# Projections spread over all eight steps of batch 0, routing moved beside batch 1, and zero rows written to the free slots alone

## The chip, the core and the metric

The kernel runs on one core of a Trainium2 chip. Its engines are TensorE (PE), VectorE (DVE), ScalarE (ACT), GpSimd (POOL) and SyncE (SP), which issues most DMAs. Each engine works off its own instructions in the order in which they are written and waits on semaphores; nothing reorders them. The metric is device time of one execution in microseconds.

## What is computed

Input x has 4 batches of 512 tokens with 256 features. The block computes `x + s * silu(f)`:

```python
xn = _layernorm(x, axis=-1)
s = _L0_attn_ref(xn, ...)
g = _silu(_L0_ffn_ref(xn, ...))
x = x + s * g
```

`s` is a gated recurrence: after an RMS norm, projections give q and k (128 wide), a decay a (16 heads of 8), v and g (256 wide). The state follows

```python
S = S * jnp.exp(gt)[..., None] + kt[..., None] * vt[..., None, :]
ot = jnp.einsum('bhk,bhkd->bhd', qt, S)
```

over the 512 tokens. Its output is normalised per head, gated by silu(g), multiplied by Wo and added; a gated MLP (704 wide) follows. `f` is a mixture of 16 experts (224 wide) of which a softmax router picks 4 for each token.

## The kernel before

**Attention.** Tokens run along the free dimension, 512 of a batch at once. A batch p needs eight projection outputs, numbered in the order Z (decay), K, V0, V1, LG (router logits), Q, G0, G1. Each is one PSUM bank of a rotation of three (`bank_of`), written by six f16 matmuls, high and low parts being kept apart (`triple`, L315). ScalarE takes out Z, K, Q, G0 and G1, VectorE V0, V1 and LG. V goes to `v_scratch` in DRAM and comes back copied over partitions as `vrep`. One recurrence step (a, u) of the eight of a batch a treats two value columns: VectorE multiplies `kv` (L951) and runs two scans `st` (L959), GpSimd multiplies by q (`product`, L529), TensorE sums over k (`read_out`, L1247). Step u's scans wait for product u-2, so the four engines form a ring. Before a batch is projected its rows are normalised by GpSimd (`normed_rows`, L510), turned by TensorE (`turn_rows`, L1215) and split into `anT` by ScalarE and VectorE (`high_rows`, `low_rows`). The decay also needs a sum by GpSimd (`decay_sum`), behind four passes of ScalarE.

**Order.** It is written out by hand. A prologue loads and splits the weights and projects batch 0. Then batch 0's steps run with the projections of batches 1 to 3 spread over them by one table: after step u come the outputs up to `STEP_ENDS[u]`.

```python
STEP_ENDS = [7, 11, 14, 17, 20, 24, 24, 24]
```

After `FIRST = 6` steps VectorE begins routing: some 35 small operations in a chain, between which `recurrences_beside_routing` puts one piece of a recurrence each (batch 0's steps 6 and 7, batch 1's 0 and 1). At the end `route_ready` says in which slot of `rows_scratch` each token's row goes for each of its four experts, and `name_tiles` says which expert owns each of 80 tiles of 128 slots. Then `turns` runs a pipeline: in iteration `it` batch it does its recurrence (a), batch it-1 its heads, Wo and second norm (b), batch it-2 its MLP (c). GpSimd scatters two of 64 groups of 128 rows in each turn that has a b, from b = 0 on. Slots that no token fills have to be zero: ScalarE issues 16 DMAs (`zero`, L636) that clear all 10240 slots during batch 0's steps, and scatters wait for them.

**Experts.** SP loads the gate and up weights, then waits for the last turn of `an2` (`tpn_ready`) and for all scatters, loads the first 16 tiles' rows (`load_rows`, L452), and then the down weights `wd` in two DMAs (`load_down`, L448). TensorE turns the first two tiles' rows before the last batch's W2 products, does the first tile's gate and up products, waits for both `wd` loads, and goes through the 80 tiles:

```python
gate_up(0, 0, e_first)
pe.wait_ge(s["wd_in"], 32)
tiles(0, True, False)
```

GpSimd adds each tile's output to `y_scratch` by an indirect DMA (L586), and a short tail combines both branches.

## Time and profile before

| what | us |
|---|---|
| median of 3 runs (lowest, highest) | 575.49 (574.5, 575.81) |
| profiled execution, its own time | 574.92 |
| its span, first to last instruction | 572.9 |
| busy: TensorE, VectorE, GpSimd, ScalarE | 429.3, 345.0, 304.7, 230.9 |
| one kv (L951), one scan (L959) on VectorE | 1.212, 1.210 |
| one v copy (L927) on VectorE | 0.688 |
| one product (L529), one decay sum (L515) on GpSimd | 2.352, 1.272 |
| 24 router matmuls (L315, 128x16), 8 turns (L1215) on TensorE | 0.75, 1.09 |
| granted TensorE clock, mean | 0.897 of full speed |

Busy time is the time in which an engine executes; where TensorE's clock is granted at half speed (1.2 instead of 2.4 GHz) the same matmuls are longer. "Idle before" in a row is the time in which the engine did nothing ahead of that instruction, with the one that ended it. DMAs have rows of their own queue (SPq, ACTq), which show the issue, not the transfer.

### The profile page before, as it was taken

What the parts mean: (1) busy time and instruction counts of PE and PEld (TensorE: products, weight loads), DVE (VectorE), ACT (ScalarE), POOL (GpSimd) and SP (SyncE); (2) the same over time, 40 slices, a digit from 0 to 9 for tenths busy, and PEclk for the clock granted to TensorE, in tenths of its full rate; (3) what the DMA queues carried; (4) which work ended last, traced back from release to release, by engine and by line L of the source; (5) the groups of instructions that cost most, each with busy time, mean ns of one, the idle gap of its engine ahead of it and who ended that gap; (6) DMA issues with size and microseconds to landing.
All of it is one profiled execution on the core that took longest, in us unless ns stands there. A gap on an engine that the chain in (4) does not pass through costs nothing.

```text
span 572.9 us, 8861 instructions
## 1 busy us (share of the span) xinstructions
PE 429.3 (75%) x2170; PEld 254.9 (44%) x2171; DVE 345.0 (60%) x613; ACT 230.9 (40%) x521; POOL 304.7 (53%) x230
## 2 busy tenths in 40 slices
PE   2479970313568798699889989999999999999400
PEld 1134320101223354255465557767767767677200
DVE  4665867999989979985755633333333333333065
ACT  0526642300133132122554525556655656566221
POOL 4052695146768468576720006656566656666535
PEclk9989996655759899899999999999999999999855
DMA  8334998745535234232988845666666666664493
GB/s 265 110 111 160 304 330 279 270 150 171 186 123 185 89 126 151 106 114 65 357 288 238 176 149 85 112 101 114 103 112 112 112 102 110 111 85 57 55 318 121
DMA packets 78616, 90.42 MB, mean 158 GB/s; under 512 B 7704, under 2 KB 66808, under 8 KB 78584
## 3 DMA queue, kind: packets, MB, share of 16 engines
q1 hardware_dynamic: 47584, 54.82, 31.6%
q0 software_dynamic: 14592, 19.47, 20.0%
q10 hardware_dynamic: 16408, 15.73, 8.5%
q8 instruction: 16, 0.26, 0.2%
q14 instruction: 16, 0.13, 0.1%
HBM read 50.66 MB, written 39.34 MB: 157 GB/s over the span
## 4 chain that ended last, share of the span: by engine, by line
PE 54%; DVE 19%; issue 9%; DMA 8%; POOL 4%; ACT 2%; ACTq 2%; SPq 0%; POOLq 0%; DVEq 0%
PE mm_ps L315 33%; PE sum_ps L315 12%; DVE st L959 4%; PE turn_ps L1276 3%; DVE kv L951 3%; PE mm_ps L1374 3%; POOL qs L529 2%; DMA rows_scratch<-zrow 2%; DMA eb<-n_L_ffn_expert_bias_dram 2%; PE sum_ps L1247 2%; DVE w_gu L1181 2%; DMA vrep<-v_scratch 1%; DMA y_scratch<-y,X 1%; ACTq L636 1%; DVE ghead L1111 1%
## 5 line engine op out<-in xcount | busy, mean ns | idle before, releaser
L586 POOL DMA_INDIRECT y_scratch<-y,X x80 | 124.3, 1554 | 126.7 <-ACT y L815 96.6
L315 PE MATMUL mm_ps<-w_gu,xT 128*128 x480 | 103.9, 352 | 1.6 <-DVEq L1159 1.5
L529 POOL TENSOR_TENSOR qs<-st,q_sb 128x1024 f32<-128x1024 f32 x32 | 75.4, 2356 | 49.0 <-DVE st L959 24.3
L1071 DVE TENSOR_TENSOR xT<-turn_ps,xT 128x256 f16<-128x256 f32 x80 | 33.9, 425 | 88.0 <-ACT xT L726 88.0
L315 PE MATMUL sum_ps<-wd,hT 112*128 x320 | 82.4, 380 | 0.0
L558 POOL DMA_INDIRECT rows_scratch<-rows,slot_u x64 | 64.0, 1001 | 27.2 <-issue 15.1
L959 DVE TENSOR_TENSOR_SCAN st<-sum_ps,kv 128x512 f32<-128x512 f32 x64 | 75.1, 1210 | 1.0
L315 PE MATMUL mm_ps<-an2T,w 128*128 128x512 f16 x264 | 65.1, 403 | 13.6 <-DVE h_mlp L1080 11.1
L1247 PE MATMUL sum_ps<-qs,sumk 128*32 128x512 f32 x128 | 38.2, 710 | 38.5 <-POOL qs L529 37.2
L315 PEld LDWEIGHTS mm_ps<-w_gu,xT 128*128 128x128 f16 x480 | 46.6, 97 | 33.0 <-issue 2.7
L1164 DVE SCALAR_TENSOR_TENSOR h<-mm_ps,X,sl 128x224 f32<-128x224 f32 x80 | 36.1, 451 | 40.9 <-ACT sl L799 40.9
L315 PEld LDWEIGHTS sum_ps<-wd,hT 112*128 112x128 f32 x320 | 54.3, 190 | 4.7 <-issue 0.2
L815 ACT ACTIVATE y<-sum_ps,X 128x256 f32<-128x256 f32 x80 | 38.0, 474 | 44.3 <-PE sum_ps L315 44.3
L799 ACT ACTIVATE sl<-mm_ps,X 128x224 f32<-128x224 f32 x80 | 35.8, 447 | 43.4 <-PE mm_ps L315 43.4
L315 PE MATMUL mm_ps<-anT,w_a 128*128 128x512 f16 x168 | 43.0, 414 | 11.2 <-DVE anT L912 9.2
L315 PEld LDWEIGHTS mm_ps<-an2T,w 128*128 128x128 f16 x264 | 26.3, 103 | 54.1 <-issue 16.6
L315 PE MATMUL mm_ps<-w,h_mlp 128*128 128x256 f32 x192 | 47.8, 394 | 1.0 <-DVE h_mlp L1080 1.0
L951 DVE TENSOR_TENSOR kv<-vrep,mm_ps 128x1024 f32<-128x1024 f32 x32 | 38.8, 1212 | 5.6 <-ACT mm_ps L677 4.1
L315 PEld LDWEIGHTS mm_ps<-w,h_mlp 128*128 128x128 f32 x192 | 33.9, 189 | 14.5 <-issue 10.0
L732 ACT ACTIVATE sg<-mm_ps 128x512 f32<-128x512 f32 (+1 forms) x24 | 14.3, 597 | 46.8 <-PE mm_ps L315 46.8
L1276 PE MATMUL turn_ps<-ident,X 128*128 128x128 f32 x160 | 30.7, 274 | 2.5 <-issue 2.5
L315 PEld LDWEIGHTS mm_ps<-anT,w_a 128*128 128x128 f16 x168 | 16.9, 105 | 34.9 <-issue 17.8
(165 smaller groups left out, 533.4 us busy)
## 6 DMA issues: line engine op xcount, KB each, us to landing
vrep<-v_scratch SPq DMA_DIRECT2D x64, 256.0 KB
rows_scratch<-zrow ACTq DMA_DIRECT2D x16, 685.0 KB, 11.7
X<-rows_scratch SPq DMA_DIRECT2D x80, 137.0 KB, 2.6
w_gu<-y_scratch SPq DMA_DIRECT2D x16, 256.0 KB, 6.1
y_scratch<-zrow ACTq DMA_DIRECT2D x6, 640.0 KB, 5.9
w_gu<-in_L_ffn_gate_proj_dram SPq DMA_DIRECT2D x16, 224.0 KB, 6.8
w_gu<-in_L_ffn_up_proj_dram SPq DMA_DIRECT2D x16, 224.0 KB, 7.1
wd<-in_L_ffn_down_proj_dram SPq DMA_DIRECT2D x1, 3136.0 KB, 17.4
```

Of the source, the lines that this page charges most:

```text
L315: last = nc.tensor.matmul(out_ap, lhsT, rhs, start=(n == 0), stop=(n == len(pairs) - 1))
L529: nc.gpsimd.tensor_tensor(qs[:, u % 2, :, :], st[:, u % 2, :, :], pair_bc(q_sb[:, TOK(a)]), ALU.mult).then_inc(s["qs_ready"], 1)
L558: nc.gpsimd.indirect_dma_start(rows_dram, bass.IndirectOffsetOnAxis(ap=slot_u[:, j, t:t + 1], axis=0), rows[:, t, :], None).then_inc(s["sc ...
L586: nc.gpsimd.indirect_dma_start(y_dram[u % 2], bass.IndirectOffsetOnAxis(ap=X[:, u, TOKEN_C:TOKEN_C + 1].bitcast(U32), axis=0), y[:, u, :], ...
L799: nc.scalar.activation(sl[:, u % 2, :], M[u % 2][:, 0:I], ACT.Silu, scale=X[:, u, SCALE_C:SCALE_C + 1])\
L815: nc.scalar.activation(y[:, u, :], sum_ps[:, u % 2, 0:D], ACT.Copy, scale=X[:, u, bass.ds(e + WEIGHT_C, 1)])\
L951: nc.vector.tensor_tensor(kv[:, r, :, :], vrep[:, r, :, :], pair_bc(K_BANK), ALU.mult).then_inc(s["kv_ready"], 1)
L959: nc.vector.tensor_tensor_scan(st[:, r, j, :], A_BANK, kv[:, r, j, :], 0.0, ALU.mult, ALU.add).then_inc(s["st_ready"], 1)
L1071: nc.vector.tensor_tensor(xT[:, u % 2, 1, :, :].rearrange("p c n -> p (c n)"), PS[u % 2][:, 0:KC * P], xT[:, u % 2, 0, :, :].rearrange("p ...
L1164: nc.vector.scalar_tensor_tensor(out=h[:, u % 2, :], in0=M[u % 2][:, I:2 * I], scalar=X[:, u, SCALE_C:SCALE_C + 1], in1=sl[:, u % 2, :], o ...
L1247: last = nc.tensor.matmul(O0[rows_at:rows_at + QUARTER, :], sumk[:, off:off + QUARTER], qs[:, u % 2, j, :], start=(dd % PER == 0), stop=(d ...
L1276: last = nc.tensor.transpose(PS[u % 2][:, n * P:(n + 1) * P], X[:, u, n * P:(n + 1) * P], ident[:, :])
```

## The change

1. The outputs' order is V0, V1, Z, K, LG, Q, G0, G1, and batch 0's projection waits for each output's own weights (`LOW_PARTS`) instead of all. Loads are split over more semaphores; five small loads move from ScalarE's queue to SP's. VectorE computes only batch 1's scales ahead of the recurrence; batches 2 and 3 follow in its steps 0 and 1, and GpSimd's rows for them after its products 0 and 1. Value loads of a batch's first four steps wait for the first half of v alone.
2. `STEP_ENDS` spreads the 24 outputs over all eight steps. `FIRST` is 8, and beside routing stand batch 1's steps 0 to 3. The counting matmuls move to batch 1's turn 2, ScalarE's exponential behind batch 0's second half.
3. The 16 clearing DMAs are gone. VectorE computes the numbers of the 2048 free slots (`pad_u`, nine small operations), and GpSimd writes `zrow` to them by 16 indirect DMAs. Scatters begin at batch 0's turn 4; batch 3's turns 0 to 3 hold five scatters and four of the new DMAs each.

```diff
@@ -275,31 +280,40 @@
-        Z_OUT, K_OUT, V0_OUT, V1_OUT, LG_OUT, Q_OUT, G0_OUT, G1_OUT = range(8)
...
+        V0_OUT, V1_OUT, Z_OUT, K_OUT, LG_OUT, Q_OUT, G0_OUT, G1_OUT = range(8)
+        LOW_PARTS = {V0_OUT: 2 * KC, V1_OUT: 2 * KC, Z_OUT: 3 * KC, K_OUT: 3 * KC, LG_OUT: 3 * KC + 1, Q_OUT: 4 * KC + 1,
+                     G0_OUT: 5 * KC + 1, G1_OUT: 5 * KC + 1}
...
-        STEP_ENDS = [7, 11, 14, 17, 20, 24, 24, 24]
+        STEP_ENDS = [4, 7, 10, 13, 16, 19, 22, 24]
@@ -318,6 +332,7 @@
+        SCATTER_FROM = 4
@@ -379,12 +394,24 @@
-            for w, col in ((Wv, VC), (Wg, GC)):
-                sp.dma_start(wa_raw[:, :, col:col + D], w.rearrange("(c p) n -> p c n", p=P)).then_inc(s["wa_in"], 16)
+            sp.dma_start(wa_raw[:, :, VC:VC + D], Wv.rearrange("(c p) n -> p c n", p=P)).then_inc(s["wv_in"], 16)
             for w, col in ((Wq, QC), (Wk, KCOL)):
-                sp.dma_start(wa_raw[:, :, col:col + QK], w.rearrange("(c p) n -> p c n", p=P)).then_inc(s["wa_in"], 16)
-            for c in range(1, B):
+                sp.dma_start(wa_raw[:, :, col:col + QK], w.rearrange("(c p) n -> p c n", p=P)).then_inc(s["wqk_in"], 16)
+            sp.dma_start(wa_raw[:, :, GC:GC + D], Wg.rearrange("(c p) n -> p c n", p=P)).then_inc(s["wg_in"], 16)
+            load_x(1)
...
+                sp.dma_start(bz[:, :], strided(bkg2, 0, [[1, KD], [KD, H], [1, 1]])).then_inc(s["bz_in"], 16)
+                for c in range(KC):
+                    sp.dma_start(bgT[:, c:c + 1], strided(bg, c * DH, [[1, DH], [HD, H], [1, 1]])).then_inc(s["bg_in"], 16)
...
+            for c in range(2, B):
                 load_x(c)
+            with nc.allow_non_contiguous_dma(reason="a few hundred numbers"):
+                sp.dma_start(ln2[:, :], ln2_w.rearrange("(c p) -> p c", p=P)).then_inc(s["late_in"], 16)
+                sp.dma_start(eb[:, :], expert_bias.rearrange("(a e) -> a e", a=1).to_broadcast((P, E))).then_inc(s["late_in"], 16)
@@ -409,9 +436,8 @@
-                if u == 0:
-                    for c in range(2):
-                        sp.wait_ge(vt_out[c], 16 * (b + 2))
+                if u % 4 == 0:
+                    sp.wait_ge(vt_out[u // 4], 16 * (b + 2))
@@ -452,7 +477,7 @@
-            sp.wait_ge(s["scatter"], 16 * NT * TOP)
+            sp.wait_ge(s["scatter"], 16 * (NT * TOP + NPAD))
@@ -541,17 +568,23 @@
+                if u == 0:
+                    pool.wait_ge(s["ln_ready"], 3)
+                if u < 2:
+                    for t in range((u + 2) * TPB, (u + 3) * TPB):
+                        normed_rows(t)
+                else:
+                    mlp_weights((u - 2) // 3, (u - 2) % 3)
@@ -559,20 +592,30 @@
+            def scatter_pads(n):
+                for _, i in zip(range(n), pads):
+                    nc.gpsimd.indirect_dma_start(
+                        rows_dram, bass.IndirectOffsetOnAxis(ap=pad_u[:, i:i + 1], axis=0),
+                        zrow[:, :], None).then_inc(s["scatter"], 16)
             def step_fn(a, b, c, u):
                 if a is not None:
                     if u == 0:
                         pool.wait_ge(s["evac_act"], len(ACT_NTH) * a + ACT_NTH[Q_OUT])
                     product(a, u)
-                if b == 0 and u == 0:
+                if b == 0 and u == SCATTER_FROM:
                     pool.wait_ge(s["route_ready"], 1)
-                    pool.wait_ge(s["zero_fill"], 16 * NT)
-                if b is not None:
+                if b == 1 and u == 0:
+                    pool.wait_ge(s["pads_ready"], 1)
+                if b is not None and (b > 0 or u >= SCATTER_FROM):
                     scatter(2)
+                if b == B - 1 and u < U // 2:
+                    scatter(3)
+                    scatter_pads(-(-NPAD // (U // 2)))
@@ -603,33 +646,36 @@
             nc.scalar.preload_act_table_set("natural_log_exp_and_others")
-            act.wait_ge(s["wa_in"], 64)
-            act.wait_ge(s["small_in"], 16 * NSMALL)
-            act.wait_ge(s["wv_ready"], 1)
+            act.wait_ge(s["ln1_in"], 16)
+            act.wait_ge(s["wqk_in"], 32)
             for c in range(KC):
-                for out_ap, in_ap in wparts(c, 0):
-                    nc.scalar.activation(out_ap, in_ap, ACT.Copy, scale=ln1[:, c:c + 1]).then_inc(s["wprep_act"], 1)
...
             act.wait_ge(s["wz_ready"], 1)
...
+            act.wait_ge(s["wv_ready"], 1)
+            for c in range(KC):
+                nc.scalar.activation(dh_view(c, 0, VC), dh_raw(c, VC), ACT.Copy,
+                                     scale=ln1[:, c:c + 1]).then_inc(s["wprep_act"], 1)
@@ -697,14 +746,8 @@
-                    zero(rows_dram[t * (SLOTS // NT):(t + 1) * (SLOTS // NT)], "zero_fill")
                 if u == 4:
                     value_half(0, 0)
-                if u == 5:
-                    act.wait_ge(s["ex_in"], 1)
-                    nc.scalar.activation(ex[:, :, :], prod[:, :, :], ACT.Exp).then_inc(s["exp_ready"], 1)
-                    act.wait_ge(s["exp_ready"], 1)
-                    nc.scalar.preload_act_table(ACT.Silu)
@@ -716,6 +759,10 @@
             value_half(0, 1)
+            act.wait_ge(s["ex_in"], 1)
+            nc.scalar.activation(ex[:, :, :], prod[:, :, :], ACT.Exp).then_inc(s["exp_ready"], 1)
+            act.wait_ge(s["exp_ready"], 1)
+            nc.scalar.preload_act_table(ACT.Silu)
@@ -928,15 +985,24 @@
+            qk_low(1)
+            dh_low(VC, 2 * KC)
             low_rows(0)
+            decay_low()
+            router_low()
+            qk_low(0)
+            dve.wait_ge(s["bz_in"], 16)
+            nc.vector.tensor_scalar(bz_neg[:, :], bz[:, :], -1.0, None, ALU.mult).then_inc(s["bz_neg"], 1)
+            take_out(0, V0_OUT)
+            dh_low(GC, 3 * KC + 1)
+            take_out(0, V1_OUT)
+            row_scales(0, TPB)
+            take_out(0, LG_OUT)
             dve.wait_ge(s["const_pool"], 1)
             step(nc.vector.tensor_scalar(head_m[:, :], head_i[:, :], H - 1, None, ALU.bitwise_and))
             nc.vector.tensor_scalar(sumk[:, P - H:P], head_m[:, :], 0.0, KS, ALU.is_equal, ALU.mult).then_inc(s["const_dve"], 1)
-            for c in range(1, B):
-                statistics(c)
-            for i in range(OUTS):
-                take_out(0, i)
-            scales(TPB, NT, TPB + NT)
+            statistics(1)
+            scales(TPB, 2 * TPB, 3 * TPB)
             low_rows(1)
@@ -962,19 +1028,27 @@
-            FIRST = 6
+            FIRST = U
+            BESIDE = 4
             for u in range(FIRST):
                 for _ in recurrence(0, u):
                     pass
+                if u == 0:
+                    row_scales(TPB, 2 * TPB)
+                    statistics(2)
+                    statistics(3)
+                if u == 1:
+                    scales(2 * TPB, NT, 6 * TPB)
+                    row_scales(2 * TPB, NT)
                 for p, i in outs_at(u):
                     if turned_before(p, i):
                         low_rows(turned_before(p, i))
                     take_out(p, i)
             def recurrences_beside_routing():
-                for a, u in ((0, FIRST), (0, FIRST + 1), (1, 0), (1, 1)):
-                    yield from recurrence(a, u)
+                for u in range(BESIDE):
+                    yield from recurrence(1, u)
@@ -1036,6 +1115,14 @@
+            of_e = lambda ap: ap.rearrange("p (a e) -> p a e", a=1).to_broadcast((P, NPAD, E))
+            step(nc.vector.tensor_tensor(past, of_e(pads_to[:, :]),
+                                         pad_no[:, :].rearrange("p (i a) -> p i a", a=1).to_broadcast((P, NPAD, E)), ALU.is_le))
+            step(nc.vector.tensor_tensor(past, past, of_e(held[:, :]), ALU.mult))
+            step(nc.vector.tensor_reduce(pad_f, past, AX.X, ALU.add))
+            step(nc.vector.tensor_tensor(pad_f, pad_f, pad_no[:, :], ALU.add))
+            nc.vector.tensor_copy(pad_u[:, :], pad_f).then_inc(s["pads_ready"], 1)
@@ -1219,6 +1306,8 @@
+                if p == 0:
+                    pe.wait_ge(s["wprep_dve"], LOW_PARTS[i])
@@ -1259,12 +1347,6 @@
-                if u == U - 1:
-                    pe.wait_ge(s["m16_ready"], 1)
-                    pe.wait_ge(s["evac_act"], len(ACT_NTH) * B)
-                    sel = M16[:, :, :].rearrange("p t e -> p (t e)")
-                    nc.tensor.matmul(M[0][:, 0:NT * E], before16[:, :], sel, start=True, stop=True)
-                    nc.tensor.matmul(M[0][:, NT * E:2 * NT * E], ones16[:, :], sel, start=True, stop=True).then_inc(s["cum_ready"], 1)
@@ -1308,6 +1390,12 @@
+                if a == 1 and u == 2:
+                    pe.wait_ge(s["m16_ready"], 1)
+                    pe.wait_ge(s["evac_act"], len(ACT_NTH) * B)
+                    sel = M16[:, :, :].rearrange("p t e -> p (t e)")
+                    nc.tensor.matmul(M[0][:, 0:NT * E], before16[:, :], sel, start=True, stop=True)
+                    nc.tensor.matmul(M[0][:, NT * E:2 * NT * E], ones16[:, :], sel, start=True, stop=True).then_inc(s["cum_ready"], 1)
```

GpSimd, from batch 2's turn 6 to the first add of an expert tile, before:

```order
L529 TENSOR_TENSOR qs<-st,q_sb 128x1024
L558 DMA rows_scratch<-rows,slot_u 10240x274 x2
L529 TENSOR_TENSOR qs<-st,q_sb 128x1024
L558 DMA rows_scratch<-rows,slot_u 10240x274 x2
L529 TENSOR_TENSOR qs<-st,q_sb 128x1024
L558 DMA rows_scratch<-rows,slot_u 10240x274 x18
L586 DMA y_scratch<-y,X 2176x256 x16
```

and after the change:

```order
L591 DMA rows_scratch<-rows,slot_u 10240x274 x2
L556 TENSOR_TENSOR qs<-st,q_sb 128x1024
L591 DMA rows_scratch<-rows,slot_u 10240x274 x7
L597 DMA rows_scratch<-zrow,pad_u 10240x274 x4
L591 DMA rows_scratch<-rows,slot_u 10240x274 x5
L597 DMA rows_scratch<-zrow,pad_u 10240x274 x4
L591 DMA rows_scratch<-rows,slot_u 10240x274 x5
L597 DMA rows_scratch<-zrow,pad_u 10240x274 x4
L591 DMA rows_scratch<-rows,slot_u 10240x274 x5
L597 DMA rows_scratch<-zrow,pad_u 10240x274 x4
L591 DMA rows_scratch<-rows,slot_u 10240x274 x4
L629 DMA y_scratch<-y,X 2176x256 x16
```

The block between the last product (`qs`) and the first `y_scratch` holds 18 DMAs before and 42 after; 16 of these take `zrow`.

TensorE, from the turn of batch 1's rows on, before:

```order
L1215 MATMUL turn_ps<-ident,rows 128x128 x8
L315 MATMUL mm_ps<-anT,w_a 128x512 x24
L315 MATMUL mm_ps<-rw,anT 128x16 x24
L315 MATMUL mm_ps<-anT,w_a 128x512 x6
L1215 MATMUL turn_ps<-ident,rows 128x128 x8
L315 MATMUL mm_ps<-anT,w_a 128x512 x30
L1247 MATMUL sum_ps<-qs,sumk 32x512 x2
L315 MATMUL mm_ps<-anT,w_a 128x512 x6
L315 MATMUL mm_ps<-rw,anT 128x16 x24
L315 MATMUL mm_ps<-anT,w_a 128x512 x6
L1247 MATMUL sum_ps<-qs,sumk 32x512 x2
```

and after:

```order
L1302 MATMUL turn_ps<-ident,rows 128x128 x8
L329 MATMUL mm_ps<-anT,w_a 128x512 x24
L329 MATMUL mm_ps<-rw,anT 128x16 x24
L329 MATMUL mm_ps<-anT,w_a 128x512 x6
L1302 MATMUL turn_ps<-ident,rows 128x128 x8
L329 MATMUL mm_ps<-anT,w_a 128x512 x6
L1336 MATMUL sum_ps<-qs,sumk 32x512 x2
L329 MATMUL mm_ps<-anT,w_a 128x512 x18
L1336 MATMUL sum_ps<-qs,sumk 32x512 x2
L329 MATMUL mm_ps<-anT,w_a 128x512 x12
L329 MATMUL mm_ps<-rw,anT 128x16 x24
L1336 MATMUL sum_ps<-qs,sumk 32x512 x2
```

The rows with 24 router matmuls mark LG. Batch 1's projection keeps its place behind the turn, but the second turn (batch 2) is now followed by one output instead of five ahead of the first read-out, and three outputs stand between read-outs from there on.

VectorE, from batch 0's step 0 to step 2, before:

```order
L951 TENSOR_TENSOR kv<-vrep,mm_ps 128x1024
L959 SCALAR_TENSOR_TENSOR st<-sum_ps,kv 128x512 x2
L927 COPY vt<-mm_ps 128x512 x2
L921 TENSOR_TENSOR lg<-mm_ps,rows 128x64
L912 TENSOR_TENSOR anT<-turn_ps,anT 128x512 x2
L951 TENSOR_TENSOR kv<-vrep,mm_ps 128x1024
L959 SCALAR_TENSOR_TENSOR st<-sum_ps,kv 128x512 x2
L927 COPY vt<-mm_ps 128x512
```

and after, first up to the aggregates, then (the reciprocal root lies between) from `shift` on:

```order
L1017 TENSOR_TENSOR kv<-vrep,mm_ps 128x1024
L1025 SCALAR_TENSOR_TENSOR st<-sum_ps,kv 128x512 x2
L921 TENSOR_TENSOR ctmp<-rsq 128x4
L922 SCALAR_TENSOR_TENSOR rows<-ctmp,nhalf 128x4
L901 BN_STATS bst<-xn 128x6 x8
L984 COPY vt<-mm_ps 128x512 x2
L1017 TENSOR_TENSOR kv<-vrep,mm_ps 128x1024
L1025 SCALAR_TENSOR_TENSOR st<-sum_ps,kv 128x512 x2
L907 BN_AGGR mv<-bst 128x2 x8
```

```order
L914 SCALAR_TENSOR_TENSOR shift<-rsq,mv 128x2x8
L921 TENSOR_TENSOR ctmp<-rsq 128x8
L922 SCALAR_TENSOR_TENSOR rows<-ctmp,nhalf 128x8
L978 TENSOR_TENSOR lg<-mm_ps,rows 128x64
L969 TENSOR_TENSOR anT<-turn_ps,anT 128x512 x2
L1017 TENSOR_TENSOR kv<-vrep,mm_ps 128x1024
```

Statistics and scales of batches 2 and 3 now stand between the recurrence's pieces, and the second `anT` split behind them.

## Rows read from the trace of the kernel before

**Rows 1.** Windows: stretch, each engine's busy us (instructions), PE clock, DMA share, GB/s.
```profile
53.04:81.55 28.51, 25.68 (x160) 10.70 (x158) 21.87 (x24) 16.11 (x29) 17.84 (x10) 1.00 0.91 312
81.55:121.65 40.10, 7.80 (x30) 2.34 (x30) 35.09 (x68) 12.00 (x18) 14.61 (x7) 0.65 0.82 275
```

**Rows 2.** Chain that ended last, prologue: start us, us, what.
```profile
6.98 9.39 DMA eb<-n_L_ffn_expert_bias_dram
```

**Rows 3.** Timeline, prologue: start us, us, engine line operation, idle before.
```profile
4.52 1.41 DVE L854 BATCH_NORM_STATS2 bst<-xn 128x6 f32<-128x256 f32 x4 [4.52 <-DMA xn<-in_L_attn_x_dram]
16.46 3.50 ACT L626 ACTIVATE w_a<-wa_raw,ln 128x256 f16<-128x256 f32 x4 [6.80 <-DMA eb<-n_L_ffn_expert_bias_dram]
23.25 7.92 PE L315 MATMUL mm_ps<-anT,w_a 128*128 128x512 f16 x24 [7.83 <-DVE anT L912]
36.14 6.48 POOL L510 TENSOR_SCALAR rows<-xn,rsq,shift 128x256 f32<-128x256 f32 x12 [6.13 <-DVEq L870]
40.67 1.21 DVE L951 TENSOR_TENSOR kv<-vrep,mm_ps 128x1024 f32<-128x1024 f32 x1
```

**Rows 4.** Timeline, projections and read-outs beside batch 0's steps.
```profile
40.85 7.66 PE L315 MATMUL mm_ps<-anT,w_a 128*128 128x512 f16 x24 [2.02 <-issue]
57.68 1.05 PE L1247 MATMUL sum_ps<-qs,sumk 128*32 128x512 f32 x4
58.67 1.47 PE L315 MATMUL mm_ps<-anT,w_a 128*128 128x512 f16 x6
81.55 1.33 DVE L985 TENSOR_TENSOR lg<-lg,eb 128x256 f32<-128x256 f32 x1 [2.47 <-PE mm_ps L315]
```

**Rows 5.** Waits of VectorE, 40 to 166 us: in total, times, longest.
```profile
DVE kv L951 <- ACT mm_ps L677: 4.1, 1, 4.1
```

**Rows 6.** Timeline, after routing; the last row is batch 3's.
```profile
125.03 1.86 DVE L1047 TENSOR_SCALAR tile_expert<-own 1x80 uint32<-1x80 f32 x1
135.02 2.79 DVE L1111 TENSOR_SCALAR ghead<-ghead 128x64 f32<-128x64 f32 x1
135.39 2.35 POOL L529 TENSOR_TENSOR qs<-st,q_sb 128x1024 f32<-128x1024 f32 x1
141.84 1.21 DVE L951 TENSOR_TENSOR kv<-vrep,mm_ps 128x1024 f32<-128x1024 f32 x1
277.48 0.20 DVE L1111 TENSOR_SCALAR ghead<-ghead 128x64 f32<-128x64 f32 x1
```

**Rows 7.** Timeline of GpSimd, end of its attention work.
```profile
269.06 0.96 POOL L558 DMA_INDIRECT rows_scratch<-rows,slot_u  x1 [0.30 <-issue]
270.33 0.96 POOL L558 DMA_INDIRECT rows_scratch<-rows,slot_u  x1 [0.31 <-issue]
288.97 1.23 POOL L558 DMA_INDIRECT rows_scratch<-rows,slot_u  x1 [0.30 <-issue]
```

**Rows 8.** Timeline, from the first row loads to the first expert tile.
```profile
300.45 7.46 SPq L452 DMA_DIRECT2D X<-rows_scratch  x16
321.26 0.60 PE L1276 MATMUL turn_ps<-ident,X 128*128 128x128 f32 x4
322.83 12.00 PE L315 MATMUL mm_ps<-w,h_mlp 128*128 128x256 f32 x48 [0.97 <-DVE h_mlp L1080]
337.55 0.41 PE L1276 MATMUL turn_ps<-ident,X 128*128 128x128 f32 x2
```

**Rows 9.** Page, DMA issues: count, KB each, median us to landing.
```profile
X<-rows_scratch SPq DMA_DIRECT2D x80, 137.0 KB, 2.6
wd<-in_L_ffn_down_proj_dram SPq DMA_DIRECT2D x1, 3136.0 KB, 17.4
rows_scratch<-rows,slot_u POOLq DMA_INDIRECT x64, 3.8
```

**Rows 10.** Windows: the row and down-weight loads, and a busier stretch.
```profile
300.45:326.00 25.55, 23.75 (x107) 13.12 (x106) 15.59 (x19) 12.42 (x18) 0.00 (x0) 1.00 0.95 230
277.00:285.00 8.00, 6.44 (x32) 2.84 (x30) 7.55 (x19) 4.00 (x6) 6.17 (x7) 1.00 1.08 383
```

138 lines of the change are left out of this document (80 added, 58 removed).

## Prediction

> **What bounds the kernel now.** I read the windows by stage first, then the chain that ended last, then the timeline of the stages that the change touches. Three stages follow each other. Beside batch 0's first six recurrence steps TensorE is the busy engine: 25.68 of 28.51 us against VectorE's 21.87 [rows 1]. In the routing stretch VectorE works 35.09 of 40.10 us and TensorE 7.80 [rows 1]. From about 300 us on TensorE hardly stops until the tiles end, so whatever delays its first expert tile (337.55 [rows 8]) moves the end by as much. The prologue is a chain of its own: ScalarE's weight copies wait until 16.46 for the last small load, which was issued at 6.98 and took 9.39 us [rows 2, 3].
>
> All sums are made against the profiled run: span 572.9 us, its own time 574.92, so 2.0 us lie around the span; the median of the runs, 575.49, is 0.57 above it.
>
> **Prologue.** ScalarE's queue now carries four loads instead of nine, and the weights of v are prepared first. VectorE ends the first normalisation at 9.2 as before (statistics at 4.52 [rows 3]), copies wk1T and centres Wv until about 11.7. Then come two v copies by ScalarE at 0.88 each (3.50 for four [rows 3]), one more VectorE remainder (0.5) and anT's two halves (1.3 after the first copy): the first projection starts at about 15.0 instead of 23.25. TensorE gives V0, V1, Z, K in 7.92 us [rows 3] and the router's product 0.75 later, at 23.8. VectorE now starts batch 1's statistics there: 0.4 for the head mask, then the same statistics and scales that took 4.52 to 9.20 for batch 0, 4.7 us, so GpSimd gets batch 1's rows at 28.9. From that start to the first kv it is 40.67 - 36.14 = 4.53 us [rows 3]. First kv at 33.4: **7.3 us earlier**. The small loads that moved to SP's queue (bz, two bgT, ln2, eb) stand ahead of W1, W3, wo and w2 and then of v's store; if they land as late as eb did, 9.4 us after issue, they still come by 17, before their first use. The bounds of this term are 4 and 9.
>
> **Batch 0's steps.** These lose ground. Step 0 costs VectorE a recurrence (3.55: kv 1.21 and two scans of 1.17, as in the table), 0.6 of row scales, 2.7 of statistics for batches 2 and 3 and the two v copies: the second kv at 41.9, its scans end at 45.5. Then stand the scales of batches 2 and 3, 3.5 us, on the path of GpSimd's rows 2, of TensorE's turn and of the remainder of anT: 49.0 + 4.5 = 53.5 for the third kv. TensorE idles about 5 us until 49.2 and restarts at G0 of batch 1 at 51.5. What is left for it until the router's last input: 16 outputs at 1.47 [rows 4] = 23.5, two router products 1.5, one turn 1.1 (table), six read-outs at 1.05 [rows 4] = 6.3, so 32.4. I add 1.8 for restarting at the low level of its clock (24 matmuls took 7.66 after a pause where four groups at 1.47 make 5.9 [rows 4]) and 1.6 for read-out 5. That one waits for GpSimd, which has batch 3's decay sum queued before product 5: Z at 77, four ScalarE passes 2.6, sum 1.3, product 2.35, so 83.3 where TensorE is there at 81.7. The bias add that opens routing starts at 51.5 + 35.8 = 87.3 instead of 81.55 [rows 4]: **5.8 later**, though two more recurrences are then done.
>
> **Routing and what follows.** It kept VectorE from 81.55 to 121.65, 40.1 us with four recurrences beside it [rows 1]. The 4.1 us wait for batch 1's K bank [rows 5] was ScalarE held by issuing zero fills; these issues are gone, about 1.1 of the wait stays while the last g is taken out. Four small operations are added (0.9). So 38.0, **2.1 less**. The five operations that find the free slots add 2.1 behind it. Two recurrences (7.0) no longer follow. Two operations were stretched by a GpSimd product: the last of the tile names took 1.86, the head scale 2.79 against 0.20 in batch 3 [rows 6]. GpSimd will have nothing to do there, since product 3 is long done and product 4 needs step 4: I take 0.2 for each, 4.3 less together (bounds 0 and 5). Sum: 7.0 + 4.3 + 2.1 - 2.1 - 5.8 = **5.5 us**: the kv of batch 1's step 4 at 136.3 instead of 141.84 [rows 6]. From there the order is the old one up to batch 3, so this stage hands on 5.5. The 7.3 of the prologue are inside it, not beside it. Bounds 0 and 10.
>
> For these stretched operations the Trainium skill (SBUF — State Buffer, the section on the two separate sides) says that VectorE and GpSimd share a port pair which one instruction holds to its end. The 2.79 beside a product that starts 0.37 us later and ends with it agrees [rows 6]. The same rule speaks against the change: more scatters run beside VectorE's work, and it could hold GpSimd's descriptors up. The old burst's mean spacing already has that in it; by it rather than by the clean spacing the sum below would be 1.4 us more.
>
> **Free-slot rows at the end of attention.** This part costs. Batch 0's first four turns scatter nothing now, so before batch 3's turns 40 scatters are issued instead of 48; 24 are left, and 16 for free slots come on top: 40 in a row where 16 stood. The 16 start at 269.06, 1.27 apart, the last at 288.97 [rows 7]. Twenty-four more at 1.27 are 30.5 us: the last starts at 319.5 and lands 3.8 later [rows 9], at 323.3. All times here are the old ones; the 5.5 are taken off at the end. SP's row loads wait for all of them; they began at 300.45 [rows 8], when another wait (the last turn of an2) ended. So they start **22.9 later**. The two first rows land at 326.4 (0.47 + 2.6 [rows 9]); TensorE turned them at 321.26 and began W2 at 322.83 [rows 8], now at 327.0: 4.2 of delay. It then stands before its wait for the down weights at 341.7. Those are issued behind 16 row loads (7.46 us) and need 17.4 [rows 8, 9]: 323.3 + 24.9 = 348.2. The second part, 0.45 MB, was issued 14 us after the first; now it is right behind it, 1.9 us at 0.24 MB per us: 350.1. The loads ran at 230 GB/s with the DMA busy 0.95 of the time [rows 10], so nothing hides here. The first tile's turn at 337.55 [rows 8] becomes 350.1: **12.5 later**. After 8 us of idleness I take the 1.8 for the low clock once more (0 to 3). Together 14.3, bounds 10 and 18. The zero fills that go (16 of 685 KB) shorten nothing: their place had one wait of ScalarE, counted above.
>
> Sum: 574.92 - 5.5 + 14.3 = 583.7; beside the median of the runs **584.3 us**.
>
> **Rivals.**
> The weights arrive in time (faster). If the 5.9 MB of rows and down weights moved at 383 GB/s, as another stretch shows [rows 10], they would take 15.3 us and be there at 339 to 340, before TensorE asks. Only the 4.2 of the two first rows would remain: 574.92 - 5.5 + 4.2 = 573.6. It decides from landing before 341.7. Against it: that stretch moved other shapes, and these loads filled the DMA at 230. Chance 0.08. The Trainium skill (DMA: Bandwidth & Descriptors, Bandwidth) gives three quarters of the peak for transfers of 1 MiB and more; an estimate by it is about 10 us for the 3.2 MB that took 17.4 here [rows 9], so the trace disagrees.
>
> The front gives more. Without TensorE's and GpSimd's waits routing could start at 83.9 (51.5 + 32.4) and the tail could cost its lower bound: 574.92 - 8.9 + 10 = 576.0. For it: my walk through the steps has many waits of 1 to 2 us. Chance 0.08.
>
> The burst is hidden altogether: row loads at their old place, 574.92 - 5.5 = 569.4. It would need scatters at half of 1.27; all in the trace stand at that or above. Chance 0.04.
>
> The front gives nothing. The stretched operations stay stretched (4.3) and one more decay sum delays a read-out (1.2): 574.92 + 14.3 = 589.2. For it: GpSimd has two decay sums inside products' way. Chance 0.18.
>
> My forecast has 0.62. Within 0.2% (1.2 us, what a measurement of this kernel can tell) of 575.49 lie most of the second rival: same 0.06; faster 0.12; slower 0.82. The range of 8 in 10 is 577 to 590.
>
> **What would show it.** First projection near 15, first kv near 33, bias add of routing near 87, batch 1's kv of step 4 near 136; the head scale 0.2 there. At the end of attention a block of 42 indirect transfers without a product between them, row loads starting more than 20 us after the last turn of an2, and TensorE with a hole of about 8 us just before the first expert tile, ended by the down weights. I am wrong if that hole is absent or under 3 us, or if batch 1's step 4 comes before 131.

## The result and the profile after

| | before | changed |
|---|---|---|
| median of 4 and 4 runs, us | 575.65 | 586.81 (585.19 to 588.25) |
| ratio | | 1.0197, 95% interval 1.0162 to 1.0231 |
| profiled run, its span, us | 574.92, 572.9 | 585.87, 583.8 |
| mean granted clock | 0.897 | 0.877 |

The changed kernel is slower by 1.6 to 2.3%. The prediction was 584.3 (577 to 590), slower, with 0.82 on it. The span grew by 10.9 us.

The front, from VectorE's timeline of the changed kernel (start, length, engine, line, operation, tiles; in brackets the idle time ahead and what ended it):

```profile
33.78 1.21 DVE L1017 TENSOR_TENSOR kv<-vrep,mm_ps 128x1024 f32<-128x1024 f32 x1
...
87.06 0.42 DVE L1059 TENSOR_TENSOR lg<-lg,eb 128x256 f32<-128x256 f32 x1 [3.04 <-PE mm_ps L329]
...
89.34 1.22 DVE L1017 TENSOR_TENSOR kv<-vrep,mm_ps 128x1024 f32<-128x1024 f32 x1 [1.86 <-ACT mm_ps L723]
...
129.24 0.19 DVE L1134 TENSOR_SCALAR tile_expert<-own 1x80 uint32<-1x80 f32 x1
...
130.60 0.20 DVE L1198 TENSOR_SCALAR ghead<-ghead 128x64 f32<-128x64 f32 x1
...
134.83 1.21 DVE L1017 TENSOR_TENSOR kv<-vrep,mm_ps 128x1024 f32<-128x1024 f32 x1
```

The first kv comes 6.9 earlier than in [rows 3], the bias add that opens routing 5.5 later than in [rows 4], the K bank is waited for 1.86 us instead of 4.1 [rows 5], and the two stretched operations of [rows 6] are at 0.2. The kv of batch 1's step 4 stands 7.0 us before its old place.

GpSimd's timeline where attention ends: the last product, the first indirect DMAs behind it, and the last of them.

```profile
259.22 2.35 POOL L556 TENSOR_TENSOR qs<-st,q_sb 128x1024 f32<-128x1024 f32 x1 [3.54 <-DVE st L1025]
261.72 1.01 POOL L591 DMA_INDIRECT rows_scratch<-rows,slot_u  x1 [0.16 <-issue]
...
264.31 0.96 POOL L591 DMA_INDIRECT rows_scratch<-rows,slot_u  x1 [0.31 <-issue]
...
317.41 0.96 POOL L591 DMA_INDIRECT rows_scratch<-rows,slot_u  x1 [0.30 <-issue]
```

There are 42 in a row, 40 of them from 264.31 to 317.41; in [rows 7] the last one starts at 288.97. What waits for them, in the timeline of SyncE's queue and TensorE:

```profile
320.20 7.47 SPq L477 DMA_DIRECT2D X<-rows_scratch  x16
...
322.48 1.17 PE L1358 MATMUL turn_ps<-ident,X 128*128 128x128 f32 x4 [5.74 <-issue]
...
323.43 14.10 PE L329 MATMUL mm_ps<-w,h_mlp 128*128 128x256 f32 x48
...
327.71 8.71 SPq L473 DMA_DIRECT2D wd<-in_L_ffn_down_proj_dram  x2
...
338.28 0.39 SPq L487 DMA_DIRECT2D xback<-in_L_attn_x_dram  x1
...
339.06 1.30 PE L329 MATMUL mm_ps<-w_gu,xT 128*128 x6 [1.53 <-DVEq L1246]
...
347.66 0.66 PE L1358 MATMUL turn_ps<-ident,X 128*128 128x128 f32 x2 [7.29 <-DMA wd<-in_L_ffn_down_proj_dram]
348.11 2.45 PE L329 MATMUL mm_ps<-w_gu,xT 128*128 x6
```

and its DMA issues in that stretch (KB each, us from issue to landing):

```profile
wd<-in_L_ffn_down_proj_dram SPq DMA_DIRECT2D x1, 3136.0 KB, 17.0
X<-rows_scratch SPq DMA_DIRECT2D x16, 137.0 KB, 3.3
xback<-in_L_attn_x_dram SPq DMA_DIRECT2D x1, 2048.0 KB, 14.1
wd<-in_L_ffn_down_proj_dram SPq DMA_DIRECT2D x1, 448.0 KB, 18.7
```

The row loads go out at 320.20 instead of 300.45 [rows 8]. The products of W2 start 0.6 later than before although the front is 4.8 ahead there, and last 14.10 instead of 12.00 because the granted clock is at its lower level after the pause of 5.74 (0.65 of full speed on the mean from 323.4 to 330, 1.00 in the kernel before). Then TensorE stands 7.29 us before the first expert tile and the down weights end the wait. The tile turns at 347.66 instead of 337.55 [rows 8]. The account of the span: -4.8 (front) + 5.4 (rows) + 2.1 (clock in W2) + 7.3 (down weights) gives +10.0 at the tile's turn, measured 10.1. Behind it 0.8 more comes on top: the first tile's six products take 2.45 instead of 1.31 at the low clock, and a pause of 0.74 that the kernel before has there falls away.

Part of the 7.3 may belong to another load. At 338.28, when W2 has ended, SyncE issues the load of x for the tail (`xback`, 2048 KB) while the down weights are still under way, and it takes 14.1 us, where it took 8.4 in the kernel before, in which they had landed. From 320.20 to 347.66 the DMA engines moved 245 GB/s, that is 6.7 MB, of which the row and down-weight loads are 5.9. An estimate from these: up to 0.8 MB of x, 2 to 3 us, went ahead of the last of the weights. No run issues that load later.

Of the 7.0 gained by batch 1's step 4 only 4.8 are left at batch 3's step 7 (kv 255.41 instead of 260.19). Of the 2.2 lost, 1.9 go at two places: 1.1 at batch 2's step 5 and 0.8 at batch 3's step 5. TensorE's timelines show both, of the changed kernel

```profile
182.39 5.30 PE L329 MATMUL mm_ps<-an2T,w 128*128 128x512 f16 x12 [5.25 <-DVE h_mlp L1167]
...
234.11 5.27 PE L329 MATMUL mm_ps<-an2T,w 128*128 128x512 f16 x12 [4.83 <-DVE h_mlp L1167]
```

and of the kernel before

```profile
189.11 4.34 PE L315 MATMUL mm_ps<-an2T,w 128*128 128x512 f16 x12 [4.73 <-DVE h_mlp L1080]
...
239.71 4.45 PE L315 MATMUL mm_ps<-an2T,w 128*128 128x512 f16 x12 [4.83 <-DVE h_mlp L1080]
```

The same twelve products ran at 1.2 GHz to their end, or nearly so, in the one (granted clock 0.50 from 182.39 to 187.60) and rose to 2.4 GHz on the way in the other, the second time after the same idle time of 4.83. No order of instructions changed there.

The first kv itself is uncertain by a microsecond or two. Nine traces have the changed kernel's prologue: the first 24 projection products start between 15.38 and 15.60 in all of them, take 6.68 to 7.95 us, and the first kv follows at 32.26 to 33.78. Five traces have the prologue of the kernel before: products of 6.84 to 7.92 us, first kv at 38.27 to 40.84. The trace above has the longest of the one (7.95) and [rows 3] the longest of the other (7.92), so the 6.9 compare like with like.

### The profile page after: what moved, and what is told of

Its sections match the earlier page's. It is cut to its first block and busy times, and to the rows that moved or that the text cites. A ratio compares the mean times of both kernels' runs of the same rounds, so it can differ in the third digit from the quotient of the medians.

```text
span 583.8 us, 8897 instructions
## 1 busy us (share of the span) xinstructions
PE 440.6 (75%) x2170; PEld 258.5 (44%) x2171; DVE 343.3 (59%) x638; ACT 230.6 (40%) x523; POOL 324.4 (56%) x247
## 5 line engine op out<-in xcount | busy, mean ns | idle before, releaser
L329 PE MATMUL mm_ps<-w_gu,xT 128*128 x480 | 105.3, 356 | 1.6 <-DVEq L1246 1.5
L329 PE MATMUL mm_ps<-an2T,w 128*128 128x512 f16 x264 | 66.4, 409 | 14.2 <-DVE h_mlp L1167 11.7
L591 POOL DMA_INDIRECT rows_scratch<-rows,slot_u x64 | 65.3, 1021 | 16.6 <-issue 15.9
L1336 PE MATMUL sum_ps<-qs,sumk 128*32 128x512 f32 x128 | 39.5, 700 | 23.5 <-POOL qs L556 23.4
L329 PE MATMUL mm_ps<-w,h_mlp 128*128 128x256 f32 x192 | 49.9, 407 | 0.0
L329 PE MATMUL mm_ps<-anT,w_a 128*128 128x512 f16 x168 | 45.9, 430 | 5.0 <-DVE anT L969 1.9
L329 PEld LDWEIGHTS mm_ps<-w,h_mlp 128*128 128x128 f32 x192 | 35.4, 197 | 14.2 <-issue 10.3
L773 ACT ACTIVATE xT<-turn_ps 128x256 f16<-128x256 f32 x80 | 30.2, 377 | 11.6 <-PE turn_ps L1358 11.4
L1358 PEld LDWEIGHTS turn_ps<-ident,X 128*128 128x128 f32 x160 | 22.6, 146 | 24.9 <-issue 17.4
```

The costliest lines, as they stand in the source:

```text
L329: last = nc.tensor.matmul(out_ap, lhsT, rhs, start=(n == 0), stop=(n == len(pairs) - 1))
L591: nc.gpsimd.indirect_dma_start(rows_dram, bass.IndirectOffsetOnAxis(ap=slot_u[:, j, t:t + 1], axis=0), rows[:, t, :], None).then_inc(s["sc ...
L1336: last = nc.tensor.matmul(O0[rows_at:rows_at + QUARTER, :], sumk[:, off:off + QUARTER], qs[:, u % 2, j, :], start=(dd % PER == 0), stop=(d ...
L1358: last = nc.tensor.transpose(PS[u % 2][:, n * P:(n + 1) * P], X[:, u, n * P:(n + 1) * P], ident[:, :])
```

## The experiments

Twelve runs, on four chips, each chip used at one time only: e1 to e4 on chip 2, e5 to e8 on chip 11, e9 to e11 on chip 1, e12 on chip 3. Which chip the first comparison ran on is not on record. One thing differs between them, and the reading of every run hangs on it. In the first comparison and in e9 to e11 batch 3 runs smoothly beside the indirect DMAs. In all the others TensorE, ScalarE and VectorE nearly stop there. I call that the crawl, and speak of chips with and without it; whether it belongs to the chip or to something else that differed at that time, these runs do not separate. It can be read off one distance: from the kv of batch 3's step 7, written kv(3,7), to the first turn of the last an2 on TensorE. This work is the same in every kernel. "Before beside it" is the kernel before measured together with the run.

| run | indirect DMAs in a row | kv(3,7) | an2 turn | distance | median us | before beside it | ratio (95%) |
|---|---|---|---|---|---|---|---|
| before | 18 | 260.19 | 298.78 | 38.6 | 575.65 | | |
| changed | 42 | 255.41 | 294.11 | 38.7 | 586.81 | 575.65 | 1.0197 (1.0162, 1.0231) |
| e9 | 2 | 262.02 | 300.61 | 38.6 | 575.81 | 575.25 | 1.0007 (0.9983, 1.0030) |
| e10 | 26 | 256.97 | 295.64 | 38.7 | 572.03 | 575.25 | 0.9949 (0.9928, 0.9969) |
| e11 | 6 | 260.54 | 299.14 | 38.6 | 574.95 | 575.25 | 0.9991 (0.9966, 1.0017) |
| e5 | 18 | 260.18 | 309.31 | 49.1 | 586.90 | 585.09 | 1.0040 (1.0004, 1.0075) |
| e7 | 18 | 258.42 | 308.66 | 50.2 | 586.04 | 585.09 | 1.0013 (0.9980, 1.0046) |
| e2 | 23 | 255.49 | 311.58 | 56.1 | 589.06 | 584.85 | 1.0064 (1.0037, 1.0092) |
| e1 | 26 | 253.49 | 313.76 | 60.3 | 591.77 | 584.85 | 1.0101 (1.0069, 1.0132) |
| e12 | 26 | 255.22 | 314.18 | 59.0 | 590.55 | 584.70 | 1.0110 (1.0077, 1.0143) |
| e8 | 26 | 253.80 | 312.69 | 58.9 | 590.50 | 585.09 | 1.0083 (1.0051, 1.0114) |
| e3 | 42 | 253.41 | 333.90 | 80.5 | 609.57 | 584.85 | 1.0402 (1.0360, 1.0445) |
| e4 | 42 | 255.86 | 335.41 | 79.6 | 610.37 | 584.85 | 1.0412 (1.0372, 1.0451) |
| e6 | 42 | 254.83 | 334.07 | 79.2 | 609.86 | 585.09 | 1.0402 (1.0375, 1.0430) |

**e1_gaps and e12_gaps_again**, the changed kernel with its indirect DMAs dealt out otherwise:

```
+            PER_TURN = [[0, 0, 0, 0, 2, 2, 4, 2], [2, 2, 2, 6, 3, 2, 4, 2], [2, 2, 2, 6, 3, 2, 4, 2], [3, 3, 3, 3, 3, 3, 3, 3]]
...
-                    scatter(2)
-                if b == B - 1 and u < U // 2:
-                    scatter(3)
-                    scatter_pads(-(-NPAD // (U // 2)))
+                    spread_rows(PER_TURN[b][u])
```

(`spread_rows(n)` issues rows as long as there are some, then zero rows.)

> The changed kernel with its 80 indirect DMAs (64 of rows, then 16 of zero rows) dealt out anew: 2, 2, 4, 2 in the last four turns of batch 0, then 2, 2, 2, 6, 3, 2, 4, 2 in the turns of batch 1 and of batch 2 (the extra ones where GpSimd stood idle 5.8, 1.9 and 3.5 us in the changed kernel's trace), and 3 in each turn of batch 3, which is left 24 instead of 40. Theory 1 (the block delays everything behind it, the front is a gain): the last of them starts near 294 instead of 317.4, the row loads go out near 296 instead of 320.2, no wait of several us for the down weights stands before the first expert tile, which turns near 333; 586.8 - 10.1 - 4.8 gives 571 to 573, some 4 us faster than the kernel before. Theory 2 (the front gains nothing that lasts, what was lost lies in the clock and in TensorE's work): 580 or more, hole or no hole. Theory 3 (GpSimd has no room in batches 1 and 2, products come late): hole gone, product of step 7 of batch 3 at 263 or later instead of 259.2; 575 to 580.

> The changed kernel with its 80 indirect DMAs dealt out as in the first run of this study (2, 2, 4, 2 in batch 0, 2, 2, 2, 6, 3, 2, 4, 2 in batches 1 and 2, 3 a turn in batch 3), once more, since the crawl of the engines beside the row of indirect DMAs, which two of the three chips show, covered what it was to tell. On a chip without the crawl, theory 1 (the long row cost what the front had gained and more): kv of step 7 of batch 3 at 255.4 as in the changed kernel, last of 26 in a row at 296, row loads near 297, first expert tile at 332.8, 4.8 before the kernel before; ratio 0.990 to 0.994 and time 569 to 572. Theory 2 (the zero rows cost time wherever they stand): no better than with the zero fills back, 572 to 574. On a chip with the crawl: ratio 1.007 to 1.013 as the first time.

Both fell on chips with the crawl, which covers the late row loads: the 571 to 573 of theory 1 were missed by 20 us, and the theories are not decided by the time. Two things can still be read. Seven extra indirect DMAs a batch fit into GpSimd's idle time: kv(3,7) is at 253.49 where e3, with the old dealing on the same chip, has 253.41. And 16 fewer in a row are worth 17.8 us on e1's chip (609.57 - 591.77, e3 standing for the changed kernel, which was not run there).

**e2_even**, as e1 with 3 in every turn.

> The changed kernel with three indirect DMAs in every turn from step 4 of batch 0 on (12 in batch 0, 24 each in batches 1 and 2, 20 in batch 3). One turn of GpSimd with a product and two of them took 4.84 us in the changed kernel's trace, with three it takes 6.1. Eight turns then need 49 us, and eight turns of the second batch stood 49.2 us apart (kv of step 4 of batch 1 at 134.8, of batch 2 at 184.0). Theory 1 (room only in the gaps): short turns of 3.5 to 4.8 us are overrun, products are late in five of eight turns and TensorE and VectorE wait for them, 3 to 8 us are lost against the run with the gaps filled; 575 to 580. Theory 2 (GpSimd is far enough ahead): the same time as with the gaps filled, 571 to 573.

GpSimd's timeline in batch 2:

```profile
181.89 2.37 POOL L556 TENSOR_TENSOR qs<-st,q_sb 128x1024 f32<-128x1024 f32 x1
184.43 1.00 POOL L591 DMA_INDIRECT rows_scratch<-rows,slot_u  x1 [0.17 <-issue]
185.74 0.97 POOL L591 DMA_INDIRECT rows_scratch<-rows,slot_u  x1 [0.30 <-issue]
187.01 0.96 POOL L591 DMA_INDIRECT rows_scratch<-rows,slot_u  x1 [0.30 <-issue]
188.00 2.37 POOL L556 TENSOR_TENSOR qs<-st,q_sb 128x1024 f32<-128x1024 f32 x1
```

A turn takes 6.11 us and GpSimd has no idle time left, as theory 1 says, but kv(3,7) is only 2.0 later than in e1, less than the 3 to 8 expected. The time is 2.7 us shorter than e1's (589.06 against 591.77) all the same: the row at the end has 23 instead of 26, and beside the crawl that counts for more (distance 56.1 against 60.3).

**e3_down_first**, the changed kernel with two row loads ahead of the down weights and fourteen behind.

> The changed kernel, its block as it is, but of the 16 row loads only two go out ahead of the big load of the down weights, the other 14 behind it. The down weights are then issued near 321.3 instead of 327.7. Theory 1 (weights are late because they are issued late): they land near 339, the wait of 7.3 us ahead of the first expert tile is 0 to 1.5, the first tile turns near 341 instead of 347.7; 579 to 581. Theory 2 (bandwidth): the loads of the rows and the weights together take the same time in any order, the hole stays above 4 us; 584 to 587.

Not told: with the crawl TensorE reaches the expert tiles so late that no weights are waited for in any order (609.57; the changed kernel 609.86 in e6). That the hole of 7.3 could be closed this way stays open.

**e4_before_late**, the kernel before with 42 of its 64 indirect DMAs in a row at the end:

```
-                if b is not None:
-                    scatter(2)
+                if b == 1:
+                    scatter(1)
+                if b == 2:
+                    scatter(2)
+                if b == B - 1 and u < U // 2:
+                    scatter(10)
```

> The kernel before with nothing changed but where its 64 indirect DMAs stand: none in batch 0, one a turn in batch 1, two in batch 2, ten in each of the first four turns of batch 3, so that 40 stand in a row at the end, as in the changed kernel. Theory 1 (the block alone makes the tail late): the block starts near 266.5 and its last one near 319 to 322, row loads near 323 to 325, a hole of 7 to 8 us before the first expert tile; 575.6 + 10.1 + 4.8 = 590.5, 587 to 592, slower than the changed kernel, whose front is 4.8 earlier. Theory 2 (the tail is late for something else in the change, the zero rows or the DMA traffic of the front): 576 to 582. Beside it: if the stretched operation on head scales at 135.0 (2.79 us) was stretched by GpSimd's indirect DMA issues, it takes 0.2 here, and kv of step 4 of batch 1 comes 2 to 4 us earlier than 141.8.

The ratio 1.0412 equals within the noise the changed kernel's 1.0402 (e6, on another chip with the crawl). Nothing of the change but the length of the row is in this kernel: the length alone makes such a loss there. The sizes expected were wrong, since the crawl sets the tail and not the row loads. The side question has an answer: the head scale took 1.46, not 0.2, with no indirect DMA near, but beside a product, with which it ends:

```profile
132.67 2.35 POOL L529 TENSOR_TENSOR qs<-st,q_sb 128x1024 f32<-128x1024 f32 x1 [1.14 <-DVE st L963]
133.61 1.46 DVE L1115 TENSOR_SCALAR ghead<-ghead 128x64 f32<-128x64 f32 x1
```

It is so everywhere. Between 90 and 262 us the 14 traces have 37 of these small operations (head scales of 128x64, tile names) that take 0.9 to 3.1 us instead of 0.2 to 0.3. Each of them ends 0.05 to 0.10 after a product of GpSimd, there is none without a product, and none that runs beside a product stays short. In 27 of the 37 the small operation even starts 0.3 to 0.7 before the product's recorded start. The kv of batch 1's step 4 is at 139.10, 2.9 before its place in e5 (141.99), but 2.6 of that stood already at the first kv (38.27 against 40.84).

**e5_before_again, e6_after_again**, both kernels unchanged.

> The kernel before, unchanged, profiled on the chip of these runs, since in the first four runs all engines stood still for 8 to 15 us at a time between 270 and 295 with no work ahead of them, while the 32 expert weight loads ran, and the kernel before took 584.9 in the median beside them instead of 575.5. Theory 1 (instruction supply: one engine has to wait for its next instructions behind the burst of loads): the same kind of stall, of 5 to 12 us in all, stands in this trace too between 270 and 300; about 585. Theory 2 (the stall belongs to the edited kernels): no stall, 575.

> The changed kernel, unchanged, on the chip of these runs. Theory 1 (stall beside the burst wherever an engine runs out of instructions in it): a stall of 8 to 25 us between 262 and 300 in its trace, part of it hidden by the late row loads (they go out at 320 anyway); 590 to 600, ratio 1.01 to 1.03. Theory 2: trace as in the first comparison, 586.8 and ratio 1.02.

The crawl is in both, so no edit makes it. (The same kernel against itself gave 1.0040, with 1.0004 to 1.0075 as interval: a ratio that is half a per cent from 1 says little.) ScalarE in e6:

```profile
270.26 0.60 ACT L779 ACTIVATE sg<-mm_ps 128x512 f32<-128x512 f32 x1 [1.13 <-issue]
271.22 0.95 ACT L832 ACTIVATE w_gu<-w_gu 128x896 f16<-128x896 f32 x1 [0.36 <-DMA w_gu<-in_L_ffn_up_proj_dram]
285.76 0.60 ACT L779 ACTIVATE sg<-mm_ps 128x512 f32<-128x512 f32 x1 [13.59 <-issue]
286.25 1.05 ACT L799 ACTIVATE gs<-g_sb 128x1024 f32<-128x1024 f32 x1
287.20 0.94 ACT L832 ACTIVATE w_gu<-w_gu 128x896 f16<-128x896 f32 x1
316.55 0.60 ACT L779 ACTIVATE sg<-mm_ps 128x512 f32<-128x512 f32 x1 [28.41 <-issue]
```

TensorE in e6:

```profile
275.34 1.78 PE L329 MATMUL mm_ps<-an2T,w 128*128 128x512 f16 x6 [2.58 <-issue]
286.41 2.74 PE L329 MATMUL mm_ps<-an2T,w 128*128 128x512 f16 x6 [9.29 <-issue]
301.27 2.74 PE L329 MATMUL mm_ps<-an2T,w 128*128 128x512 f16 x6 [12.11 <-issue]
317.20 2.74 PE L329 MATMUL mm_ps<-an2T,w 128*128 128x512 f16 x6 [13.19 <-issue]
```

TensorE starts 0.65 to 0.75 us after ScalarE's sg (285.76, 316.55) and VectorE's gating (h_mlp, 300.52) start: it is not late itself. Those three are. By the program the first needs a product that ended by 272.8, the second only the sg that ended at 286.4, the third a product that ended at 277.1, and ScalarE was free from 288.1. GpSimd's last indirect DMA starts at 313.42, and from 316.55 on all is smooth again. In the trace of the first comparison the same steps take their normal time beside the same row. The windows of e6 (PE, PEld, DVE, ACT, POOL busy, clock, DMA share, GB/s) show the weight loads end near 295 and the stop go on:

```profile
280.00:290.00 10.00, 2.74 (x6) 0.74 (x6) 0.61 (x1) 2.38 (x3) 7.66 (x8) 0.50 1.08 385
290.00:300.00 10.00, 0.00 (x0) 0.00 (x0) 0.00 (x0) 0.00 (x0) 7.56 (x9) 0.50 0.63 231
300.00:310.00 10.00, 2.74 (x6) 0.74 (x6) 2.88 (x4) 0.00 (x0) 7.56 (x9) 0.50 0.30 110
```

**e7_before_few, e8_gaps_few**, at most 8 of the 32 expert weight loads under way:

```
             for e in range(E):
+                if e >= 4 and e % 2 == 0:
+                    sp.wait_ge(raw_in[e // 2 - 2], 64)
                 load_gate_up(e)
```

> The kernel before, with one thing changed: the queue that issues the 32 expert weight loads of 224 KB waits, before each group of four from the third on, until the group two ahead of it has landed, so that at most 8 are under way instead of all 32. Theory 1 (the instruction supply waits behind the queued loads): no engine stands still for more than 3 us with nothing to wait for; 573 to 577, faster than the kernel before on this chip by 8 to 10. Theory 2 (the stall has nothing to do with the depth of the burst): stalls as before, 585.

> The changed kernel with the indirect DMAs dealt out as in the first run of this study (2, 2, 4, 2 / 2, 2, 2, 6, 3, 2, 4, 2 twice / 3 a turn) and the expert weight loads at most 8 at a time. If both causes are found (theory 1 on the block, and instruction supply behind the burst), nothing late is left and the front's gain stays: row loads near 296, no hole before the first expert tile, 570 to 573, and 4 to 5 us faster than the kernel before with the same throttled loads. If the front's gain is not real: 575 to 578 with both.

No effect: distances of 50.2 (49.1 in e5) and 58.9 (59.0 in e12, 60.3 in e1). Theory 1, that instructions are supplied late because the loads queue so deep, is refuted as far as the depth goes. Nor would it explain e6 after 295. The trace of e6 has two transfers of instructions between 262 and 322, one at about 275 and one between 302 and 303, both just after VectorE has taken up work again (274.60, 300.52), while there are three stops. The Trainium skill (Runtime: NRT & Kernel Launch, Instruction fetch mechanics) says that an engine's instructions are refilled in blocks of 16 KiB by a DMA queue of its own and that crossing such a block is mostly hidden; whether it is here, no run shows.

**e9_before_early**, the kernel before with none of its indirect DMAs in batch 3.

> The kernel before with its 64 indirect DMAs dealt out as 2, 2, 2, 2, 2, 2, 4, 2 in batch 0 and 2, 2, 2, 6, 3, 2, 4, 2 in batches 1 and 2, none in batch 3. In the repeated profile of the kernel before, TensorE, ScalarE and VectorE crawled from 273 to 291 (about 10 us lost) and took up speed again 1.5 us after the last of the 18 indirect DMAs in a row (289.6); in the changed kernel the crawl ended at 317.2, 2.8 us after the last of 42 (314.4). Theory 1 (the crawl hangs on the indirect DMAs in a row beside the weight loads): no wait over 3 us between 262 and 300, row loads near 300, 575 to 577, ratio 0.982 to 0.986. Theory 2 (the burst of weight loads alone makes it): crawl to the end of the loads at 290 as before, 585. Theory 3 (GpSimd has no room in batches 1 and 2): the products come late, 578 to 582.

The chip had no crawl, so theory 1 was not put to the test. On such a chip taking the row away gains nothing: with 2 instead of 18 it takes 575.81, ratio 1.0007. The new dealing loses 1.8 at kv(3,7) (1.1 of it at batch 2's step 5, where TensorE's clock rose late here too), and the profiled span is 1.7 longer; the distance is 38.6 in both.

**e10_fill_back**, the free-slot rows undone: ScalarE's zero fills back, the 16 indirect DMAs of zero rows and their arithmetic out.

> The changed kernel with one of its three parts undone: the zero rows are again written by ScalarE's 16 large zero fills in batch 0, the 16 indirect DMAs of zero rows and the arithmetic for their numbers are out. 26 instead of 42 indirect DMAs stand in a row at the end. Theory 1 (each indirect DMA in the row costs its 1.27 us at the end): 16 x 1.27 = 20 us earlier end of the row, and the part of the crawl that it held: 609.9 - 14 to 20 = 590 to 596. Beside it the arithmetic for the numbers (2.1 us of VectorE at 124) goes, and ScalarE issues 16 fills beside the projections. Rival (the fills, 9 MB, hold up the loads of the values and K bank): 596 to 600.

The chip had no crawl; against the changed kernel's 586.81, measured where before took 575.65, it takes 572.03 where before took 575.25. So this one part costs 14.4 us (586.81 - 572.03 - 0.4 between the two befores), by runs at two times. GpSimd's and TensorE's timelines:

```profile
296.54 0.96 POOL L589 DMA_INDIRECT rows_scratch<-rows,slot_u  x1 [0.30 <-issue]
```

```profile
318.12 0.60 PE L1336 MATMUL turn_ps<-ident,X 128*128 128x128 f32 x4
319.69 12.00 PE L329 MATMUL mm_ps<-w,h_mlp 128*128 128x256 f32 x48 [0.97 <-DVE h_mlp L1145]
333.25 1.31 PE L329 MATMUL mm_ps<-w_gu,xT 128*128 x6 [1.56 <-DVEq L1224]
334.42 0.41 PE L1336 MATMUL turn_ps<-ident,X 128*128 128x128 f32 x2
```

The row starts 1.6 later than the changed kernel's and ends 20.9 earlier, so it is 22.4 shorter, 1.40 for each of the 16. Row loads go out at 299.06, 1.8 after the last turn of an2 has ended: the row still holds them a little, but that is hidden. There is no pause before W2 and no hole before the first tile, which turns 13.2 before the changed kernel's and 3.1 before [rows 8]. These 3.1 are the front's: kv(3,7) is 3.2 before its place in the kernel before, though about 1 of that may be the prologue's clock (24 products in 6.84 here, 7.92 in [rows 3]). The fills cost the front something: VectorE waits for the K bank again,

```profile
94.47 1.22 DVE L1008 TENSOR_TENSOR kv<-vrep,mm_ps 128x1024 f32<-128x1024 f32 x1 [3.91 <-ACT mm_ps L713]
```

and of these 5.1 us (89.34 in the changed kernel) 2.5 are left at batch 1's step 4, since the arithmetic for the free slots is gone too, and 1.6 at kv(3,7), the two groups of twelve products taking 4.94 and 4.45 here instead of 5.30 and 5.27.

**e11_fill_early**, e10 with 6 in a row instead of 26:

> The changed kernel with the zero fills back as in the run before this, and the 64 indirect DMAs dealt out as 2, 2, 4, 2 from step 4 of batch 0, 2, 2, 2, 7, 3, 3, 4, 2 in batches 1 and 2 and 1, 1, 1, 1 in batch 3: the new front without the old tail. Theory 1 (front worth 4.8 to 7 us, row of indirect DMAs the rest): no crawl, row loads near 294 to 296, first expert tile near 331; 569 to 573 and 3 to 7 us faster than the kernel before with none in batch 3. Theory 2 (the front gives nothing): the same time as that kernel. Theory 3 (10 extra indirect DMAs a batch are too many for GpSimd beside the products): 575 to 580.

574.95, ratio 0.9991. By the time alone theory 2 would do as well as theory 3; the trace decides for the third. kv(3,7) is at 260.54, 3.6 later than in e10: nine extra indirect DMAs in each of two batches use up the front's gain, and nothing is won back, since 26 in a row held no engine up.

**The fastest version is e10**, on a chip without the crawl: 0.9949 (0.9928 to 0.9969) of the kernel before. The interval is clear of 1 and the trace shows the gain at the first tile, but it is hardly more than the 0.4% that one kernel differed from itself. It was not run on a chip with the crawl. There its 26 in a row would stand beside e1's, and e1 lost to the kernel before by 1.0%.

## Why the prediction was right

- **Prologue.** 15.0 and 33.4 were forecast for the first projection and the first kv; 15.47 and 33.78 came, 6.9 us earlier instead of 7.3. Second and third kv: 41.9 and 53.5 against 42.07 and 53.76. That the kv agree to 0.4 is in part luck: the sum took 7.92 for the first 24 products, which take 6.68 to 7.95 by where the clock rises. The small loads were no limit, as the sum had it. (The sum's two scans of 1.17, said to be the table's, are 2.34; by the table's 1.210 they are 2.42, which changes nothing.)
- **Bias add** 87.3, measured 87.06, with TensorE as the engine waited for (3.04) and its wait for product 5 (2.50 at 81.63), behind batch 3's decay sum, as forecast.
- **Routing and what follows.** From the bias add to the kv of step 4 I had 49.0 us; it took 47.8. The wait for the K bank was held by the zero fills' issues, as the step said: e10 brings them back and the wait with them (3.91). Tile names and head scale went to 0.2, and the products stretch them, as the step said (37 of 37 cases, under e4).
- **Front handed on unchanged.** Here the step failed. 7.0 was gained at step 4 against 5.5 forecast. The order is the old one from there, but that does not hand the gain on: 2.2 were given back, 1.9 of them at two places where TensorE's clock rose later. 4.8 arrived at the end of attention. The term was right within 0.7 by two errors of opposite sign, which is luck, and the clock is the one to learn from.
- **The row of indirect DMAs.** 42 without a product between them, as forecast; mean spacing of the 40 (317.41 - 264.31) / 39 = 1.36 instead of 1.27, because six of them were stretched to 1.2 to 1.9. The row of the kernel before has such ones too: (288.97 - 269.06) / 15 = 1.33, so "1.27 apart" was its common spacing and not its mean, and the prediction's own 1.4 us for the difference belonged in the sum. The last started 3.4 later than forecast (314.0 with the front taken off): 0.75 because the row began later, 2.7 by the spacing. It landed 2.8 after its start instead of 3.8. Row loads 320.20 against 317.9.
- **Hole before the first tile.** 8.4 forecast, 7.29 measured, ended by the down weights; the smaller second load (448 KB) took 18.7 us and landed last, as reckoned. That the load of x shares the DMA engines with them from 338.28 on was in no term. First tile: 12.5 - 5.5 = 7.0 later forecast, 10.1 measured; the whole: 12.5 + 1.8 - 5.5 = 8.8 forecast, 10.9 measured in the span. The 2.1 too little are 0.7 of front, 1.2 of later first rows (5.4 against 4.2) and 2.1 + 0.8 - 1.8 = 1.1 of clock, less 1.0 of hole.
- **Low clock.** One term of 1.8 was too little and stood at the wrong place: it was put behind the hole, where 0.8 came, and nothing was put on W2, which lost 2.1 after a pause of 5.74 that the sum had reckoned as delay only.
- **Tail in all.** 14.3 forecast; measured 10.9 + 4.8 = 15.7 in the trace, and 14.4 by undoing the part (e10), which also gives the fills back. Both are inside 10 to 18.
- **Rivals.** Weights in time, burst hidden: refuted by the hole and by row loads 19.8 later. Front gives nothing: refuted, 4.8. The front gives more: refuted, since it wanted routing to begin at 83.9 and it began at 87.06; the 7.0 at step 4 came from elsewhere (routing 1.2 shorter than reckoned, bias add 0.24 earlier).
- **Not foreseen.** On three of four chips the kernel before takes 585 us. The changed kernel, run on one of these, takes 610, and the change costs 4.0% instead of 2.0%. There the loss comes with the same row but by another way: the last an2 turn itself is late (334.07), the row loads go out when it has ended (335.74) although the last indirect DMA started at 313.42, and no hole stands before the first tile.

## What to carry to other kernels

Where one engine's DMA issues form a row at the end of a stage, count them and multiply by the spacing in the trace (1.27 to 1.36 us here): 9 MB of zeros less (11.2 filled before, 2.2 written now) cost 16 issues, 22 us of row, and 14.4 us of time. Look at what else waits at that place before shortening it further; on the chip without the crawl 26 in a row cost nothing, 42 did, 6 gained nothing more, while on the others already 18 come with 10 us. Measure a change of this kind on more than one chip, and compare with a run of the kernel before on the same chip.

## What the runs showed of the hardware that was not expected

- **The crawl.** On three of four chips ScalarE and VectorE start late after all that they wait for is there, by 12.3 us in e5 (sg at 290.49, its product done by 276.81 and ScalarE free from 278.18) and by 13.0, 14.2 and 28.4 us in e6, while GpSimd's indirect DMAs stand in a row in batch 3. The distance of the table grows by 10.5 (11.6 in e7), 17.5, 21.7 (20.4, 20.3) and 41.9 (41.0, 40.7) us for 18, 23, 26 and 42 in a row: about 1.27 us, one DMA's spacing, for each beyond the first ten. So it ends with the row, whatever its length. It doesn't hang on the depth of the weight loads (e7, e8), nor on their running at all (e6 after 295). In batches 1 and 2, where products stand between them, two to six do no such harm. What makes the engines slow, and why not on every chip, stays open. So does whether the row makes the crawl or only sets its end: a kernel without a row there was run only on the chip without the crawl.
- **The clock of TensorE** rose in the middle of a group of twelve products in one kernel and at its end or later in the other, the second time after the same idle time of 4.83 us (4.45 against 5.27). In e10 the first of the groups took 4.94 after an idle time of 5.82. So the length of the pause before does not decide it alone. 1.9 us of a gain won upstream were lost by that, with no change of order.
- **A small VectorE operation is held to the end of a GpSimd product**, also when it starts up to 0.69 us before the product's recorded start: 0.2 us became 0.9 to 3.1 in 37 of 37 cases. Thirteen others that start 0.69 to 0.9 before it stay at 0.2.
- **The same prologue has several lengths.** The first kv of the kernel before is at 38.27, 39.37, 39.76, 40.67 and 40.84 in the five traces with its prologue. Between 38.27 (e4) and 40.67 half is the last small load, behind which ScalarE starts at 15.12 in the one and at 16.46 in the other, and half the clock: the first 24 products take 6.84 and 7.92.
- **The stretched ones in a row of indirect DMAs stand at fixed places.** The 16th takes 1.86 to 1.87 and the 18th 1.23 in the traces of the kernel before, of the changed one and of e10, the 24th 1.35 in the latter two, whatever they write (rows or zero rows). Why is open.
- **Landing times of a small load behind a large one.** 448 KB took 18.7 us issued right behind 3136 KB and beside the load of x, and 7.4 in the kernel before, where 13.5 us lay between them.
